# Windowed attention block: the output projection by channel half of a half image, one product for the statistics' totals, and the weights' scale from a matmul

## What is computed

```python
def _forward(x, Wq, Wk, Wv, Wo, bo, pos_emb, scale):
    xh = x.transpose(0, 2, 3, 1)
    q = xh @ Wq; k = xh @ Wk; v = xh @ Wv
    q2, k2, v2 = (win(q), win(k), win(v))        # (b, 64 places, head, 16 windows, 28)
    sim = jnp.einsum('bmhid,bmhjd->bmhij', q2 * scale, k2) + pos_emb
    attn = jax.nn.softmax(sim, axis=-1)
    o = jnp.einsum('bmhij,bmhjd->bmhid', attn, v2)
    o = o @ Wo + bo                              # back in image order
    ...
def _gn(v, G=16, eps=1e-5):                      # v: (b, 32, 32, 224)
    g = v.reshape(B_, H_, W_, G, C_ // G)
    m = jnp.mean(g, axis=(1, 2, 4), keepdims=True)
    s = jnp.var(g, axis=(1, 2, 4), keepdims=True)
    return ((g - m) / jnp.sqrt(s + eps)).reshape(v.shape)
x = x + _L0_conv_ref(_gn(x), Wq, Wk, Wv, Wo, bo, pos_emb, scale)
```

## Time and profile before

| | |
|---|---|
| median of 3 runs | 3698.62 us (3698.57 to 3699.42) |
| the profiled execution | 3697.35 us |
| its span, first to last instruction | 3695.5 us |
| TensorE matmuls busy | 98% of the span |
| VectorE busy | 82% |
| ScalarE busy | 81% |
| GpSimd busy | 55% |
| mean granted TensorE clock | 0.998 of full speed |

### The profile page before, as it was taken

One profiled execution on the slowest core, in us unless ns is written; L12 is line 12 of the kernel. 1 busy time (PEld: TensorE's weight loads), 2 busy tenths in 40 slices (PEclk: granted clock), 3 DMA queues, 4 the chain that ended last, 5 costly groups with the idle time before them and its releaser, 6 DMA issues.

```text
span 3695.5 us, 167632 instructions
## 1 busy us (share of the span) xinstructions
PE 3631.9 (98%) x68096; PEld 2649.5 (72%) x68096; DVE 3027.3 (82%) x5028; ACT 2982.9 (81%) x5377; POOL 2018.0 (55%) x3207
## 2 busy tenths in 40 slices
PE   5999999999999999999999999999999999999998
PEld 3777777777777777777777777777777777777766
DVE  6888888888888888888888888888888888888875
ACT  6888888888888888888888888888888888888874
POOL 4555555555555555555555555555555555555553
PEclk9999999999999999999999999999999999999999
DMA  4555555555555555555555555555555555555544
GB/s 94 138 144 136 145 142 141 138 146 141 138 141 146 142 136 143 144 144 134 144 144 142 134 147 141 142 137 149 138 139 143 144 141 137 144 144 142 135 127 112
DMA packets 252112, 513.67 MB, mean 139 GB/s; under 512 B 62672, under 2 KB 63120, under 8 KB 251536
## 3 DMA queue, kind: packets, MB, share of 16 engines
q1 hardware_dynamic: 250000, 504.35, 52.3%
q10 hardware_dynamic: 1536, 0.07, 0.0%
HBM read 118.31 MB, written 117.44 MB: 64 GB/s over the span
## 4 chain that ended last, share of the span: by engine, by line
PE 96%; issue 1%; POOL 1%; SPq 1%; DVE 1%; ACT 1%; DMA 0%; POOLq 0%; ACTq 0%; DVEq 0%
PE ps_out L323 20%; PE ps_q L323 18%; PE ps_k L323 18%; PE ps_v L323 16%; PE ps_o L366 14%; PE ps_s L354 11%; PE ps_tot L420 1%; ACT xn L477 0%; SPq L270 0%; POOL sc L712 0%; SPq L298 0%; POOL xlo L720 0%; POOL newton L694 0%; DMA p_bd<-pt_f 0%; DVE sc L646 0%
## 5 line engine op out<-in xcount | busy, mean ns | idle before, releaser
L477 ACT ACTIVATE xn<-x_sb,norm_add,norm_mul 112x128 f32<-112x128 f32 x2048 | 1017.3, 600 | 12.8 <-POOL norm_add L705 11.3
L712 POOL TENSOR_TENSOR sc<-sc,mx 128x512 f32<-128x512 f32 x512 | 536.7, 1048 | 893.7 <-DVE mx L653 893.7
L724 POOL TENSOR_TENSOR sc<-sc,rs 128x512 f32<-128x512 f32 x512 | 536.8, 1049 | 622.6 <-DVE rs L673 622.6
L323 PE MATMUL ps_out<-ohi,wo_s 128*112 128x256 f16 x4096 | 722.4, 279 | 2.2 <-DVE x_sb L629 2.2
L323 PE MATMUL ps_q<-xhi,wqk 112*128 112x512 f16 x2048 | 610.9, 380 | 12.4 <-POOL xlo L720 10.6
L323 PE MATMUL ps_k<-xhi,wqk 112*128 112x512 f16 x2048 | 609.4, 379 | 0.0
L641 DVE TENSOR_TENSOR olo<-ps_o,ohi 128x512 f16<-128x512 f32 x512 | 353.3, 690 | 310.6 <-ACT ohi L519 301.6
L366 PE MATMUL ps_o<-p_bd,v_sb 128*32 128x128 f32 x16384 | 554.5, 276 | 7.6 <-DMA p_bd<-pt_f 6.5
L323 PE MATMUL ps_v<-wv_s,xhi 112*128 112x224 f16 x4096 | 560.4, 259 | 1.5 <-issue 1.5
L720 POOL TENSOR_TENSOR xlo<-xn,xhi 112x1024 f16<-112x1024 f32 x256 | 548.2, 2141 | 13.7 <-ACT xhi L488 13.7
L494 ACT ACTIVATE q_sb<-ps_q 128x512 f32<-128x512 f32 x512 | 305.4, 597 | 281.3 <-PE ps_q L323 270.2
(11 more groups left out here) (74 smaller groups left out, 5852.5 us busy)
## 6 DMA issues: line engine op xcount, KB each, us to landing
k_bd<-k_cut SPq DMA_DIRECT2D x1024, 128.0 KB
p_bd<-pt_f SPq DMA_DIRECT2D x2048, 64.0 KB, 2.5
x_sb<-in_x SPq DMA_DIRECT2D x256, 448.0 KB, 4.5
out_y<-x_sb SPq DMA_DIRECT2D x256, 448.0 KB, 3.5
k_cut<-in_L_conv_Wq SPq DMA_DIRECT2D x2, 98.0 KB
k_cut<-in_L_conv_Wk SPq DMA_DIRECT2D x2, 98.0 KB
k_cut<-in_L_conv_Wv SPq DMA_DIRECT2D x2, 98.0 KB
pt_f<-in_L_conv_Wo SPq DMA_DIRECT2D x8, 24.5 KB
```

What stands on the lines that cost most here:

```text
L323: last = nc.tensor.matmul(dst, w_parts(a, ch), x_parts(c, ch), start=(n == 0), stop=(n == 3 * chunks - 1))
L477: nc.scalar.activation(xn[:, b % 2, :, c4, :, :, nw].rearrange("p r c q -> p q r c"), x_sb[:, b % XBUFS].rearrange("p ch (nh r w) -> p (ch ...
L712: nc.gpsimd.tensor_tensor(rows, rows, mx[:, t % 2].unsqueeze(2).broadcast_to(by_row), ALU.subtract).then_inc(shifted, 1)
L724: nc.gpsimd.tensor_tensor(rows, rows, rs[:, t % 2].unsqueeze(2).broadcast_to(by_row), ALU.mult).then_inc(probs, 1)
```

## The change

- The output projection: instead of 256 tokens for both channel halves (twice six matmuls of 256 columns), a call does 512 tokens, a half image, for one channel half (six matmuls of 512 columns). Step g = 2h makes channel half 0 of half image h, step 2h + 1 makes half 1. As a half image must be complete first, `OUT_LAG` goes from 3 to 4 and `FINAL_LAG` from 4 to 5; the low part keeps its place under the new name `LO_LAG = 3`. `ohi` and `olo` have four buffers instead of two.
- `add_out` works on the same 512 columns, of one channel half; the store of channel half 0 waits for step 4b + 2, that of half 1 for 4b + 3. Their calls stay the same.
- The totals: GpSimd adds the two channel halves of the sums (`join`, 112 x 32) and TensorE makes one product of it instead of two.
- The weights' scale: instead of the maximum over partitions by GpSimd, TensorE adds the 128 per-partition maxima with a matrix of ones. The sum is a bound of the maximum; the factors take 12 more bits (`W_BITS`) for it. The magnitudes are now taken by VectorE after its call t = -11 instead of before it.

The diff, cut to its core:

```diff
-PV_LAG, OUT_LAG, FINAL_LAG, STORE_LAG = 2, 3, 4, 7
+PV_LAG, LO_LAG, OUT_LAG, FINAL_LAG, STORE_LAG = 2, 3, 4, 5, 7
+        both = sb("both", [CP, 2, 2 * G])
-        ohi = sb("ohi", [128, 2, T2 * HG, WIN, WS], F16)
+        ohi = sb("ohi", [128, OBUFS, T2 * HG, WIN, WS], F16)
...
-                per_step(sp, final, 4 * b + 3, i)
+                per_step(sp, final, 4 * b + 2 + ch, i)
...
                 g = t - OUT_LAG
                 if is_step(g):
-                    per_step(pe, o_lo, g, i)
+                    h, ch = divmod(g, 2)
+                    n = 2 * h % OBUFS
+                    per_step(pe, o_lo, 2 * h + 1, i)
                     per_step(pe, final, g - 1, i)
-                    for ch in range(CH):
-                        last = split_product(
-                            ps_out[0:CP, ch * 256:ch * 256 + 256].rearrange("p (nh t y) -> p nh t y", nh=NW, t=T2),
-                            lambda a, hg: wo_s[:, a, hg, ch * CP:(ch + 1) * CP],
-                            lambda c, hg: o_parts[c][:, g % 2, hg::HG].rearrange("p t (nh nw) c -> p nh t (nw c)", nh=NW), HG)
-                    last.then_inc(projected, 1)
+                    split_product(
+                        ps_out[0:CP, :].rearrange("p (nh r y) -> p nh r y", nh=NW, r=HROWS),
+                        lambda a, hg: wo_s[:, a, hg, ch * CP:(ch + 1) * CP],
+                        lambda c, hg: o_parts[c][:, n:n + 2, hg::HG].rearrange(
+                            "p g t (nh nw) c -> p nh (g t) (nw c)", nh=NW), HG).then_inc(projected, 1)
                 b = image_at(t, TOT_LEAD)
                 if b is not None:
-                    per_image(pe, summed, b, i, 2 * CH)
+                    per_image(pe, joined, b, i)
                     wait(pe, stats, STAT_OPS * (b - 1) + 1, i, STAT_OPS * XBUFS)
-                    for ch in range(CH):
-                        last = nc.tensor.matmul(ps_tot[0:CP, :], ones[:, :], part[:, b % 2, ch],
-                                                start=(ch == 0), stop=(ch == CH - 1))
-                    last.then_inc(totals, 1)
+                    nc.tensor.matmul(ps_tot[0:CP, :], ones[0:CP, 0:CP], both[:, b % 2],
+                                     start=True, stop=True).then_inc(totals, 1)
+
+            def bound_weights():
+                pe.wait_ge(w_absmax, 4)
+                nc.tensor.matmul(ps_out[:, 0:4], ones[:, :], w_max[:, :], start=True, stop=True).then_inc(w_bounded, 1)
...
-            rounds(pe, step, before_4=weights_split)
+            rounds(pe, step, before_11=bound_weights, before_4=weights_split)
...
-                    per_step(act, projected, g - 2, i)
-                    nc.scalar.activation(ohi[:, g % 2], in_x_order(ps_o[:, :]), ACT.Copy).then_inc(o_hi, 1)
+                    per_step(act, projected, 2 * ((g - OBUFS) // 2) + 1, i)
+                    nc.scalar.activation(ohi[:, g % OBUFS], in_x_order(ps_o[:, :]), ACT.Copy).then_inc(o_hi, 1)
...
-                factor(nc.vector.tensor_scalar(w_top[:, :], w_top[:, :], 2.0 ** -100, None, ALU.max))
+                factor(nc.vector.tensor_scalar(w_top[:, :], ps_out[:, 0:4], 2.0 ** -100, None, ALU.max))
...
-            rounds(dve, step, before_11=largest_weights, before_10=split_weights)
+            rounds(dve, step, before_10=split_weights)
...
+            def join(b, i):
+                if b is None:
+                    return
+                per_image(pool, summed, b, i, 2 * CH)
+                per_image(pool, totals, b - 2, i)
+                nc.gpsimd.tensor_tensor(both[:, b % 2], part[:, b % 2, 0], part[:, b % 2, 1], ALU.add).then_inc(joined, 1)
...
+                join(image_at(t, TOT_LEAD), i)
                 if is_step(t):
                     per_step(pool, inverted, t, i)
...
-            pool.wait_ge(w_absmax, 4)
-            nc.gpsimd.partition_all_reduce(w_top[:, :], w_max[:, :], 128, bass.bass_isa.ReduceOp.max).then_inc(w_allmax, 1)
```

More of the change, by code:

```diff
@@ L36 @@
 X_SCALE = 16.0
+W_BITS = 12
 PASSES = ((0, 0), (0, 1), (1, 0))
@@ L121, in build @@
         pos_in = sc[:, 0, 0:HEADS * 32].rearrange("p (h c n) -> p h c n", c=2, n=WIN)
-        ones = sb("ones", [CP, CP])
+        ones = sb("ones", [128, 128])
         ps_qk = (ps("ps_q", [128, HTOK]), ps("ps_k", [128, HTOK]))
@@ L140, in build @@
         pos_spread = sem("pos_spread")
-        w_allmax = sem("w_allmax")
+        w_bounded = sem("w_bounded")
         w_factor = sem("w_factor")
@@ L147, in build @@
         summed = sem("summed")
+        joined = sem("joined")
         totals = sem("totals")
@@ L534, in _, with split_weights @@
             dve.wait_ge(zeroed, N_ZEROED)
-            def largest_weights():
+            def split_weights():
                 dve.wait_ge(weights_loaded, 16 * N_WEIGHTS)
@@ L540, in largest_weights @@
                                             apply_absolute_value=True).then_inc(w_absmax, 1)
-            def split_weights():
-                dve.wait_ge(w_allmax, 1)
+                dve.wait_ge(w_bounded, 1)
                 n_factor = 0
@@ L553, in split_weights @@
                 exponent = 0x7F800000
-                factor(nc.vector.tensor_scalar(w_top[:, :], w_top[:, :], 2.0 ** -100, None, ALU.max))
+                factor(nc.vector.tensor_scalar(w_top[:, :], ps_out[:, 0:4], 2.0 ** -100, None, ALU.max))
                 factor(nc.vector.tensor_scalar(w_pow[:, :], w_top[:, :].bitcast(I32), exponent, None, ALU.bitwise_and))
-                factor(nc.vector.tensor_scalar(alpha[:, :], w_pow[:, :], -1.0, float((254 - 1) << 23), ALU.mult, ALU.add))
-                factor(nc.vector.tensor_scalar(unscale[:, :], w_pow[:, :].bitcast(F32), 0.125, None, ALU.mult))
+                factor(nc.vector.tensor_scalar(alpha[:, :], w_pow[:, :], -1.0, float((254 - 1 + W_BITS) << 23), ALU.mult, ALU.add))
+                factor(nc.vector.tensor_scalar(unscale[:, :], w_pow[:, :].bitcast(F32), 2.0 ** (-3 - W_BITS), None, ALU.mult))
                 factor(nc.vector.tensor_tensor(s_scale[:, :], unscale[:, 0:1], unscale[:, 1:2], ALU.mult))
@@ L608, in group_sums @@
                 if ch == 0:
-                    per_image(dve, totals, b - 2, i)
+                    per_image(dve, joined, b - 2, i)
                 nc.vector.tensor_reduce(part[:, b % 2, ch, 0:G], x_sb[:, b % XBUFS, ch].rearrange(by_group, g=G, w=WW // G),
@@ L622, in add_out @@
                     return
-                b = g // 4
+                b, ch = g // 4, g % 2
                 per_step(dve, projected, g, i)
@@ L626, in add_out @@
                     per_image(dve, bias_added, b, i, CH)
-                r0 = (g % 4) * T2
-                xr = x_sb[:, b % XBUFS].rearrange("p ch (nh y) -> p (ch nh) y", nh=NW)[:, :, r0 * WW:(r0 + T2) * WW]
+                r0 = (g // 2 % 2) * HROWS
+                xr = x_sb[:, b % XBUFS, ch].rearrange("p (nh y) -> p nh y", nh=NW)[:, :, r0 * WW:(r0 + HROWS) * WW]
                 nc.vector.scalar_tensor_tensor(
-                    xr, ps_out[0:CP, :].rearrange("p (q y) -> p q y", q=CH * NW),
+                    xr, ps_out[0:CP, :].rearrange("p (nh y) -> p nh y", nh=NW),
                     out_scale[0:CP, :], xr, ALU.mult, ALU.add).then_inc(final, 1)
@@ L636, in step @@
                 stat_op(stat_b, 0, i)
-                g = t - OUT_LAG
+                g = t - LO_LAG
                 if is_step(g):
                     per_step(dve, o_hi, g, i)
-                    nc.vector.tensor_tensor(olo[:, g % 2], in_x_order(ps_o[:, :]), ohi[:, g % 2],
+                    nc.vector.tensor_tensor(olo[:, g % OBUFS], in_x_order(ps_o[:, :]), ohi[:, g % OBUFS],
                                             ALU.subtract).then_inc(o_lo, 1)
```

3 lines of the change are left out of this document (2 added, 1 removed).

## The result

The changed kernel takes 3738.49 us (3732.28 to 3739.7), the kernel before 3698.62 in the same runs: ratio 1.0104, 95% interval 1.009 to 1.0118. It is slower by 1%, where 3662.4 was forecast. The profiled execution has a span of 3736.7 us, 41.2 more than before.

What follows compares the result with a forecast made beforehand. TensorE's matmul stream was taken as the bound. 3697.35 - 32.2 (steady part) - 5.0 (start) + 1.0 (end) = 3661.2 us profiled, 3662.4 as median of runs; range 3653 to 3671, forecast's chance 0.71.

Steps and rivals of the forecast that it cites:

- TensorE's stream is the time, and an edit is worth what it takes out of the distances between matmul starts: Whole kernel: TensorE holds 96% of the chain, so savings are read from matmul start distances.
- the slower one: Rival at the totals: each join pays cold times, TensorE waits 0.57 us an image, 70 us in all: 3732 us, chance 0.03.
- The wide projection, 18 ns a step: Output projection: six wide matmuls save 3 ns each, 9.2 us over 512 steps; the first load's 45 ns stays.
- The totals, 0.32 to 0.13: Totals on TensorE: one product instead of two takes 0.13 us instead of 0.32, saving 24.3 us over 128 images.
- the steady sum: Steady part: wide projection 9.2 plus totals 24.3 gives 33.5 us, times 0.96 is 32.2 us saved.
- The join covered by 2.3 us: GpSimd before the totals: the added join, taken as 0.25 us, fits in 2.3 us of cover and costs nothing.
- VectorE has a per-image reserve of 2.2 us: VectorE's waits for the totals: 2.2 us an image of reserve against 0.26 us by which TensorE becomes shorter.
- The start, 5.0 us: Before the first `ps_q`: without GpSimd's special operation it comes near 35.8 instead of 40.84, 5.0 us earlier, bounds 0 and 5.7.
- the 7.32 us: GpSimd's idle gap at the start, read as the return from the special operation to ordinary ones; it goes with that operation.
- from the squares to the first `ps_q` it is 6.1 us, and this stays: Start: ScalarE's squares move to 29.7, and adding an unchanged 6.1 us puts the first `ps_q` at 35.8.
- The rival on the start: Start: the 7.32 us fall on image 0's join, first `ps_q` about 42.5, 1.7 later; 3667 to 3669 us, chance 0.15.
- The end, 1.0: Kernel's end: one more round of projection and add, offset by an earlier store, costs 1.0 us, bounds 0 and 2.4.

Runs made afterwards that it cites:

- after_h158: The changed kernel with only TensorE's loop moved, by padding its head to slot 158 of a 256-instruction fetch block: 3673.01 us, ratio 0.9936 to the kernel before.
- bias_late_h158: The changed kernel, TensorE's loop head at slot 158, with ScalarE's two bias additions moved behind the copy to `ohi`: 3659.76 us, ratio 0.99 to the kernel before.
- tot_only_h148: Kernel before plus only the GpSimd join and one product for the totals, TensorE's loop head at slot 148: 3687.7 us, ratio 0.9974 to the kernel before.
- before_h195: The kernel before with only TensorE's loop head moved to slot 195, closing branch at slot 66: 3754.3 us, ratio 1.0159 to the kernel before.
- wscale_only: Kernel before plus only the weights' scale by matmul: 3771.86 us with loop head at slot 130 (closing branch slot 1), 3695.47 at 108 (branch slot 235).
- slot 47: Closing branch's place in the changed kernel with only TensorE's loop head moved, to slot 229: 3734.68 us, ratio 1.0106 to the kernel before.

## Why the prediction was wrong

- **"TensorE's stream is the time, and an edit is worth what it takes out of the distances between matmul starts"**: right, but this step failed as the prediction used it: the sum put the loop's closing branch at nothing, without saying so, and the edit moves it. Shortening a loop of 6527 instructions moves its closing branch against the fetch blocks. The kernel before lay well by the chance of its length, with branches of 0.36 us; the changed one has branches of 3.3 us, of which 1.9 show between the matmuls, a second stop, and behind 5 of 19 edges the lower clock: 3.4 us a round and 69 us in all (3444.2 against 3375.4 us in after_h158). No rival had it, and the slower one (the join on TensorE's way, 3732) would have given nearly the measured time for a reason that isn't there: TensorE waits for the join twice, both times in the start.
- **The wide projection, 18 ns a step**: 15 measured (1354 to 1339), and the 45 ns of the first load stayed (424 ns against 379), as argued. Right.
- **The totals, 0.32 to 0.13**: right, 326 to 129 ns. With the back edge and the circle out of the way (bias_late_h158) the 20 rounds take 3365.9 us, 31.8 less than before's 3397.7; the steady sum had 31.4 for them.
- **The join covered by 2.3 us**: it starts at 1492.78, takes 0.25 us and is over 1.8 us before the totals at 1494.85. Covered.
- **"VectorE has a per-image reserve of 2.2 us"**: this step failed, at a price of 13 us. The wait for the totals measures what VectorE has left in that one call, not the slack of the circle through ScalarE and GpSimd, which is 28.28 - 28.10 = 0.18 us an image and smaller than the 0.26 that was taken out. The rows to read were the exponential's starts, from one image to the next.
- **The start, 5.0 us**: 1.5 measured. Where the 7.32 us go was right (the join at 10.24 takes 0.25 us, cold; the next at 12.76). The step that failed is "from the squares to the first `ps_q` it is 6.1 us, and this stays": it is 39.38 - 29.33 = 10.05, since GpSimd's queue, not ScalarE, sets `xlo` once ScalarE is early. And the rest would have been worth about 1 us.
- **The rival on the start** (the gap belongs to the first ordinary operation) doesn't hold: in the changed kernel the join is that operation and has no gap. The time it feared did come about in tot_only_h148, which has both the join and the reduction over the partitions. Its GpSimd:

```profile
16.16 0.39 POOL L751 PARTITION_ALL_REDUCE w_top<-w_max  x1 [8.47 <-DVE w_max L551]
23.41 0.24 POOL L699 TENSOR_TENSOR both<-part 112x32 f32<-112x32 f32 x1 [6.86 <-issue]
```

 The gap stands behind the special operation and falls on whatever is next, here the join of image 0: its first `ps_q` is at 48.92, 8.1 us later than before. Right behind the special operation, ahead of the gap, the trace keeps a pair of instructions called MODIFY_POOL_CONFIG (16.51 and 16.54 us here, 16.15 and 16.18 in the kernel before); the changed kernel has one pair alone, at 7.65 and 7.68, and its join starts 2.6 us behind it. The late start is the larger part of why the one product for the totals gained 10 us there and not 24; the smaller is the circle, which holds the median image at 28.10 us, so that the 20 rounds gain 18.2 us (3397.7 to 3379.5) where 0.197 x 120 = 23.6 were due. The gap is also why removing the reduction belongs to the change.
- **The end, 1.0**: from the start of the last `ps_o` (3724.70) to the end of the span it is 11.96 us, 11.49 before. 0.5, inside the bounds. The last add does stand 2.4 us further from the last weighted values (3732.07 - 3724.70 = 7.37 against 3689.02 - 3684.03 = 4.99), as forecast.

The account of the spans: 3736.7 for the changed kernel; 66.1 less when only moved (3670.6, after_h158); 13.8 less with the bias late (3656.8); 0.6 less with `xlo` first (3656.2). The forecast had 3661.2 - 1.85 = 3659.4 for it. What makes the last 3 us I haven't followed.

## What to carry to other kernels

Before an edit that adds or removes instructions in a long loop on an engine that is the bound, look at how long its closing branch takes, and afterwards look at it first; compare kernels with the branch placed alike, or the place is measured instead of the edit. Look at the granted clock behind each stop, too: a stop can cost more than its own length. A wait of another engine is no reserve of that engine's loop: follow the circle of waits that leaves out the bounding engine, take its period from the starts of one operation, and hold it against the new period of the bounding engine. A gain at the start counts only if the engine then still waits for nothing in its first steps.

## What the runs showed that was not expected

One and the same loop on TensorE (24 steps, some 6200 to 6500 instructions) costs 2.4 to 4.0 us a round more or less by its place, 56 to 76 us of 3700: (3446.4 - 3397.7) / 20 for before_h195, (3476.6 - 3397.0) / 20 for wscale_only. A branch of 1.4 to 1.6 us is nearly free here. A second stop of some 1.4 us in the first `ps_v` comes with slot 47 and the changed kernel's own, and none with slots 1 and 66; with slot 1 the `ps_v` behind the edge is 1.1 us longer because the clock is low. And an ordinary operation that is the first of its kind on GpSimd took 0.25 us at 10.24, while behind the special one the gap was 6.9 to 7.3 us and operations some steps behind it were long as well (3.14 and 1.55 us in tot_only_h148, at 30.55 and 33.77).
